# Two more tiles of x1 turned by VectorE in 32 by 32 blocks and by eight stores and two loads, instead of by TensorE

## The reference

```
x1  = layernorm(x  + causal_attention(x) @ Wo)              # 16 heads of 64, rotary positions
x2  = layernorm(x1 + softmax(x1 @ ctx^T) @ ctx)             # one head of 1024 features, per batch
out = layernorm(x2 + x2 @ W^T + bias + lora(x2))            # rank 16, an adapter chosen per batch
```

## Time and profile before

| | |
|---|---|
| median of 3 runs | 523.17 us (522.85 to 523.24) |
| profiled execution: its own time | 521.92 us |
| profiled execution: span, first to last instruction | 519.9 us |
| TensorE (PE) busy with matmuls | 511.7 us, 98% of the span |
| VectorE (DVE), ScalarE (ACT), GpSimd (POOL) busy | 324.4, 262.1 and 158.7 us |
| mean granted TensorE clock | 0.997 of full speed |
| packets of all transfers | 48358, of which 13224 under 512 bytes |

### The profile page before, as it was taken

One profiled execution on the slowest core, in us unless ns is written; L12 is line 12 of the kernel. 1 busy time (PEld: TensorE's weight loads), 2 busy tenths in 40 slices (PEclk: granted clock), 3 DMA queues, 4 the chain that ended last, 5 costly groups with the idle time before them and its releaser, 6 DMA issues.

```text
span 519.9 us, 7807 instructions
## 1 busy us (share of the span) xinstructions
PE 511.7 (98%) x2848; PEld 436.5 (84%) x2848; DVE 324.4 (62%) x695; ACT 262.1 (50%) x664; POOL 158.7 (31%) x142
## 2 busy tenths in 40 slices
PE   8999999999999999999999999999999999999995
PEld 5888888888989888888978888888787888888884
DVE  4742000177776868677774788778888786855432
ACT  5623210183846648384565356367767575535231
POOL 0003500536353554742005450115657010120010
PEclk9999999999999999999999999999999999999998
DMA  8907612431021111100097677579788685842011
GB/s 281 319 20 181 183 40 82 130 115 49 32 63 62 42 40 43 42 2 0 1 254 189 142 204 216 148 211 303 200 258 212 171 230 178 222 122 98 1 76 46
DMA packets 48358, 67.70 MB, mean 130 GB/s; under 512 B 13224, under 2 KB 31016, under 8 KB 48320
## 3 DMA queue, kind: packets, MB, share of 16 engines
q1 hardware_dynamic: 47648, 66.68, 44.9%
q10 hardware_dynamic: 672, 0.52, 0.3%
HBM read 55.13 MB, written 4.72 MB: 115 GB/s over the span
## 4 chain that ended last, share of the span: by engine, by line
PE 94%; DVE 2%; DMA 2%; ACT 1%; POOL 1%; issue 0%; SPq 0%; DVEq 0%; ACTq 0%
PE bank L576 30%; PE bank L693 28%; PE bank L587 15%; PE bank L783 6%; PE bank L603 3%; PE bank L618 3%; PE bank L814 2%; PE bank L816 2%; PE bank L819 2%; PE bank L755 1%; DMA cf_raw<-ctx_feat 1%; PE bank L767 1%; DMA x_raw<-x_feat 1%; PE bank L724 1%; PE bank L726 1%; PE bank L798 0%
## 5 line engine op out<-in xcount | busy, mean ns | idle before, releaser
L576 PE MATMUL bank<-x_hi,w_hi 128*128 128x512 f32 (+1 forms) x256 | 93.6, 365 | 0.0
L576 PE MATMUL bank<-x_hi,w_lo 128*128 128x512 f32 (+1 forms) x256 | 93.1, 364 | 0.0
L576 PE MATMUL bank<-x_lo,w_hi 128*128 128x512 f32 (+1 forms) x256 | 93.0, 363 | 0.0
L1435 DVE STREAM_TRANSPOSE prob_t<-prob 32x256 f32<-32x256 f32 x160 | 69.7, 436 | 12.1 <-ACT prob L989 9.4
L1819 POOL TENSOR_TENSOR w_lo<-w_mix,w_hi 128x1024 fp32r<-128x1024 f32 x16 | 38.3, 2395 | 104.5 <-ACT w_hi L961 104.5
L693 PE MATMUL bank<-wo,act_hi 128*128 128x512 f32 x224 | 70.2, 394 | 0.0
L693 PE MATMUL bank<-ffn,act_hi 128*128 128x512 f32 x224 | 69.7, 392 | 0.0
L979 ACT ACTIVATE prob<-prob,shift 112x112 f32<-112x112 f32 x128 | 47.8, 377 | 40.8 <-DVE shift L1418 40.8
L1832 POOL TENSOR_TENSOR norm<-norm,minus_half 128x1 f32<-128x1 f32 (+1 forms) x22 | 16.6, 754 | 135.5 <-DVE norm L1508 135.5
L576 PEld LDWEIGHTS bank<-x_hi,w_hi 128*128 128x128 f32 x256 | 48.1, 188 | 6.0
L576 PEld LDWEIGHTS bank<-x_lo,w_hi 128*128 128x128 f32 x256 | 48.1, 188 | 5.1
(11 more groups left out here) (123 smaller groups left out, 961.5 us busy)
## 6 DMA issues: line engine op xcount, KB each, us to landing
cf_raw<-ctx_feat SPq DMA_DIRECT2D x32, 376.0 KB, 4.7
ct_raw<-ctx_tok SPq DMA_DIRECT2D x24, 448.0 KB
w_raw<-qkv_w SPq DMA_DIRECT2D x16, 512.0 KB, 3.5
half_raw<-wo_w SPq DMA_DIRECT2D x16, 256.0 KB, 6.0
half_raw<-ffn_w SPq DMA_DIRECT2D x16, 256.0 KB, 6.6
wv_raw<-qkv_w SPq DMA_DIRECT2D x15, 256.0 KB, 7.4
x_raw<-x_feat SPq DMA_DIRECT2D x7, 448.0 KB, 8.2
out<-y_t SPq DMA_DIRECT2D x6, 512.0 KB, 4.4
```

The source lines that it names most:

```text
L576: last = pe.matmul(to[:, 0:cols.stop - cols.start], a[:, k, :], b[:, k, cols], start=(k == 0 and b is x_hi and a is w_hi[w]), stop=(k == K ...
L1435: return dve.transpose(quads(prob_t_wide[r], key, query), quads(prob_wide[r], query, key))
```

## The change

Tiles 5 and 6 of x1 take the way of the blocks too; batches 3 and 5 of x2 stay on it. `turn_tile(5)` and `turn_tile(6)` go from TensorE's list, and `round_turned` and `rest_turned` of a5 and a6 become `round_blocks` and `rest_blocks`.

- VectorE turns the blocks of tile 5, then later of tile 6, from `x_t[i % 4]` into `x_t[3]`, whose own tile has been used. It first waits that tile 3 has been read, and for tile 6 that the four stores of tile 5 have landed.
- Four stores of 128 KB per tile, each from 32 partitions and in runs of 32 elements (128 bytes), put the blocks in their turned places in DRAM, and one load of 512 KB in runs of 128 elements (512 bytes) brings the tile back into the bytes of `act_lo`, where ScalarE and VectorE make `act_hi` and `act_lo` of it.
- `keep_y(0, 0)` now also waits until tile 6's stores have landed.
- The lists of SyncE, ScalarE, VectorE and GpSimd are put in another order from about 340 us on. In SyncE's: the context rows of batch 2 ahead of the first `load_ff`, `load_cf(15)` and `load_cf(16)` ahead of `load_ff(6)` and `load_ff(7)`; `save_blocks("a5")` behind `load_cf(19)`, `load_blocks("a5")` ahead of `load_cf(22)`, `save_blocks("a6")` behind it and ahead of the context rows of batch 4; then `load_cf(23)`, `load_cf(24)`, the store of batch 3, and the load of tile 6.

```diff
-TURNS = ["a0", "a1", "a2", "b0", "a3", "b1", "a4", "b2", "a5", "a6", "b4", "b6", "b7"]
+TURNS = ["a0", "a1", "a2", "b0", "a3", "b1", "a4", "b2", "b4", "b6", "b7"]
-BLOCKS = [3, 5]
+BLOCKS = ["a5", "a6", "b3", "b5"]
...
+        act_raw = at("act_raw", [P, KT, B * S], A0 + 28672)
+        tile_blocks = x_t[3]
...
+            def save_blocks(name):
+                at_q, i = blocks_before(name), int(name[1:])
+                sp.wait_ge(swapped, at_q + 1)
+                if at_q:
+                    sp.wait_ge(saved, saved_after(BLOCKS[at_q - 1]))
+                if name[0] == "a":
+                    for q in range(QUADS):
+                        sp.dma_start(blocks_out[at_q][:, :, QUAD * q:QUAD * q + QUAD].rearrange(
+                                         "k (d r) t -> r (k d) t", d=QUADS),
+                                     tile_blocks[QUAD * q:QUAD * q + QUAD, :].rearrange(
+                                         "r (m t) -> r m t", t=QUAD)).then_inc(saved, 16)
...
+            def load_blocks(name):
+                at_q, i = blocks_before(name), int(name[1:])
+                sp.wait_ge(saved, saved_after(name))
+                if at_q:
+                    sp.wait_ge(moved, moved_after(BLOCKS[at_q - 1]))
+                if name[0] == "a":
+                    sp.dma_start(act_raw[:, :, tile_of(i)],
+                                 blocks_out[at_q].rearrange("k p t -> p k t")).then_inc(moved, 16)
...
             cross_mix(3)
-            turn_tile(5)
             ffn(1, 0, 4)
...
             cross_mix(4)
-            turn_tile(6)
             ffn(1, 1)
...
-                    act.wait_ge(turned, 2 * AT_TURN[f"a{i + 3}"] + 2)
+                    wait_tile_read(act, i + 3)
+                    if i == 0:
+                        act.wait_ge(saved, saved_after("a6"))
...
+            def swap_blocks(name):
+                i = int(name[1:])
+                if name[0] == "a":
+                    dve.wait_ge(x1_ready, i + 1)
+                    wait_tile_read(dve, 3)
+                    for b, which in copies_of(3):
+                        dve.wait_ge(row_in[which][b % ROWS], piece_in(b, which))
+                    if blocks_before(name):
+                        dve.wait_ge(saved, saved_after(BLOCKS[blocks_before(name) - 1]))
+                    dve.transpose(tile_blocks[:, :], x_t[i % 4][:, :]).then_inc(swapped, 1)
```

More of the change, by code:

```diff
@@ L316, in cf_before, with blocks_before, saved_after, moved_after @@
             return m - 3 if m < 7 else m - 2
-        def blocks_before(b):
-            return BLOCKS.index(b)
+        def blocks_before(name):
+            return BLOCKS.index(name)
+        def saved_after(name):
+            return sum(64 if n[0] == "a" else 16 for n in BLOCKS[:blocks_before(name) + 1])
+        def moved_after(name):
+            return sum(16 if n[0] == "a" else 64 for n in BLOCKS[:blocks_before(name) + 1])
+        def block_feat(name):
+            i = int(name[1:])
+            if name[0] == "a":
+                return act_raw[:, :, tile_of(i)], tile_of(i)
+            return x2_turned[i % ROWS][:, :, 0:S], tokens_of(i)
+        def wait_row_free(engine, b):
+            if f"b{b}" in BLOCKS:
+                engine.wait_ge(block_rest, 2 * blocks_before(f"b{b}") + 2)
+            else:
+                engine.wait_ge(turned, 2 * AT_TURN[f"b{b}"] + 2)
+        def wait_tile_read(engine, i):
+            if f"a{i}" in BLOCKS:
+                engine.wait_ge(swapped, blocks_before(f"a{i}") + 1)
+            else:
+                engine.wait_ge(turned, 2 * AT_TURN[f"a{i}"] + 2)
         def weight(of, n, k, part):
@@ L418, in copy_row @@
                              ).then_inc(row_in[which][b % ROWS], 16)
[L420 to L433, removed]
+            def save_blocks(name):
[9 more added lines that the diff above has]
+                                         "r (m t) -> r m t", t=QUAD)).then_inc(saved, 16)
+                else:
+                    sp.dma_start(blocks_out[at_q].rearrange("k p f -> p k f"),
+                                 x2_turned[i % ROWS]).then_inc(saved, 16)
@@ new lines, in load_blocks @@
+            def load_blocks(name):
[6 more added lines that the diff above has]
+                                 blocks_out[at_q].rearrange("k p t -> p k t")).then_inc(moved, 16)
+                else:
+                    for d in range(QUADS):
+                        sp.dma_start(x2_turned[i % ROWS][QUAD * d:QUAD * d + QUAD, :, :].rearrange(
+                                         "p k (q t) -> p (k q) t", q=QUADS),
+                                     blocks_out[at_q][:, :, QUAD * d:QUAD * d + QUAD].rearrange(
+                                         "k (q j) t -> j (k q) t", q=QUADS)).then_inc(moved, 16)
@@ L498, in _ @@
             load_ct(2, 2)
+            load_ff(0)
+            load_ff(1)
+            load_ff(2)
             load_ff(3)
@@ L544, in _ @@
             load_cf(29)
+            copy_row(6, 0)
+            copy_row(6, 1)
             copy_row(7, 0)
@@ L1241, in _ @@
             round_cf(19)
+            norm_x1(6)
             round_ff(11)
+            round_ct(23)
             round_cf(20)
@@ L1306, in _ @@
             round_ct(42)
+            norm_x2(6)
             round_ct(43)
-            norm_x2(6)
-            keep_y(3, 1)
             keep_cprob_t(7)
@@ L1313, in _ @@
             round_ct(46)
-            norm_y(3)
+            keep_y(3, 1)
             round_turned("b6")
             round_ct(47)
+            norm_y(3)
             keep_t_part(2)
@@ L1653, in _ @@
             add_wo(6)
+            rest_turned("a1")
             cross_top(0)
-            rest_turned("a1")
+            rest_ct(0)
             rest_cf(4)
-            rest_ct(0)
             rest_ct(1)
@@ L1701, in _ @@
             rest_cf(16)
+            cross_top(3)
+            add_wo(12)
+            rest_ct(17)
             rest_cf(17)
-            cross_top(3)
-            rest_ct(17)
-            add_wo(12)
             add_row(2)
```

181 lines of the change are left out of this document (91 added, 90 removed).

## The result

The changed kernel takes 525.18 us (median of 6 runs, 524.65 to 526.04); the kernel before, run beside it, takes 522.54 us. The ratio is 1.0054, with a 95% interval of 1.004 to 1.0067: slower by about 2.8 us. The forecast was 521.6 us, in a range that ended at 524.7. The profiled execution took 524.65 us, span 522.5 us at a mean granted clock of 0.995; that of before had a span of 519.9.

What follows compares the result with a forecast made beforehand. TensorE's list was taken as the bound (94% of the chain). -0.5 at `cross_score(5, last)`, -0.87 for tile 6 and -0.25 from 367 us gave -1.6 on the 523.17 median: 521.6 us, range 520.5 to 524.7.

Steps and rivals of the forecast that it cites:

- All hold: Other places fed by the queue, a5's tile, `keep_y(0, 0)`, batch 3's blocks: ready in time, each under a microsecond to spare.
- the rests change only their source, 0.65 us each as now: On VectorE: two more block turns of 1.24 us each, while the rests of a5 and a6 keep their 0.65 us.
- Nothing in the change leaves TensorE idle for long, so it costs nothing: TensorE's granted clock stays at 1.00, the 2.4 GHz level, with no cost.
- Two blocks, -1.74: Two eight-transpose blocks leave TensorE's list at 0.87 us each, the sure part of the gain.
- The queue: Transfers of 3.3 + 2.0 + 3.3 us delay `cf` part 23 to 411.5; `cross_score(5, last)` waits 0.8 us, starting at 413.3.
- The pause at `add_low`: At 401.81 us, TensorE's wait for VectorE's low-rank part shrinks from 0.72 to 0.3 us.
- The pause at 367 us: TensorE's wait for `cf` part 15, now rounded and loaded earlier: 0.25 of its 0.27 us gained.
- Rival 1: Transfers are hidden: stores overlap or cost 2.5 us, part 23 lands by 410.4; -2.4, 520.8 us, chance 0.15.
- rivals 3 and 4: Dearer transfers: each at its longest landing, 524.7 us, chance 0.11; short-run stores at double cost, 528.3 us, chance 0.07.
- Rival 2: Gain given back: part 23 lands at 412.6 or tile 6's stores delay `keep_y(0, 0)`; -0.5, 522.7 us, chance 0.27.
- rival 3: Three transfers each cost their longest landing, 11.7 us together; part 23 lands at 414.6; +1.5, 524.7 us, chance 0.11.
- the longest new pause stands elsewhere: Sign of being wrong: longest new pause at `cross_mix(3)` (VectorE), `ffn(0, 1)` (the bank) or `ffn(2, 0)` (batch 3's blocks).

Runs made afterwards that it cites:

- b3_first: Changed kernel with batch 3's four block loads ahead of two thirds of batch 5's context rows in SyncE's list: 523.97 us, ratio 1.0044.
- pool_in: Changed kernel with one added wait: VectorE lets GpSimd finish batch 4's scale and shift before the rest of tile 6: 521.88 us, ratio 0.9994.
- mended: Changed kernel with the edits of pool_in and b3_first, and the low-rank part kept and masked earlier: 523.02 us, ratio 1.0023, one 2919 us execution left out.
- same_again: The changed kernel word for word, measured once more: 524.28 us, ratio 1.0039 to the kernel before.
- long_runs: Changed kernel with stores of a5 and a6 in 512-byte runs, leaving out the moving of blocks within a tile: 522.95 us, ratio 1.0016.
- b3_last: Changed kernel with batch 3's four block loads behind the last third of batch 5's context rows: 525.53 us, ratio 1.0066.
- b3_ahead: b3_first with batch 3's blocks rounded and their rests taken ahead of batch 4's normalisation, GpSimd unprotected: 523.32 us, ratio 1.0018.
- pool_in_b3: Changed kernel with the edits of both pool_in and b3_first: 523.28 us, ratio 1.0015.

## Why the prediction was wrong

**The step that failed** is the sentence on batch 3's blocks: they "land near 426 and are ready near 428; `ffn(2, 0)` wants them at 429.86 - 0.5 - 0.87 = 428.5" and, of all of them, "All hold". I went from the landing straight to the rest and added 2 us, and left out what stands ahead of the rounding in ScalarE's list: `norm_x2(4)`, and with it GpSimd. The rest was done at 430.74 in place of 428, TensorE waited 2.11 us where I had none, and b3_first shows that a landing at 421.39 changes nothing in it. The landing was wrong too, 427.91 in place of 426. The held GpSimd operation hid that, but by itself it would have left about 1.1 us of the pause (see pool_in), so "All hold" would have failed without GpSimd as well.

Behind it is a smaller sentence: "the rests change only their source, 0.65 us each as now". Their own duration is as I had it (687 against 652 ns). But the source was what mattered, to a neighbour: from a bank to SBUF, and GpSimd's operation goes from 0.55 to 3.89 us. The trace of before had the sign: the same operation at line 1832 took 0.55 us as a rule and 1.84 us at 334.50. I priced the instruction and not what runs beside it.

**"Nothing in the change leaves TensorE idle for long, so it costs nothing"** fell with it: 1.59 us in the profiled execution. Over the executions: of twelve of b3_first five had a granted clock of 0.991 to 0.995 and spans of 522.9 to 525.3 us, seven had 0.996 to 0.999 and 520.9 to 522.0; of ten of pool_in, none was below 0.997. That the pause brings the fall is argued from this and from its place behind the pause in three profiles (the changed kernel, b3_first, mended); same_again, long_runs and b3_last have such a pause and no fall, and one of the twelve executions of b3_ahead, whose longest pause was 0.80 us, has a clock of 0.995. No run separates the two.

**The other terms.** Two blocks, -1.74: right, as the account shows. The queue: right. The share was 1.00 from 380 to 401 and 0.91 from 401 to 406 us, part 23 landed at 411.36 (predicted 411.5, of which the half microsecond to report stood on no row), and `cross_score(5, last)` started at 413.52 (413.3) after 0.79 us of pause (0.8). The stores cost what I had taken for them: in the trace 3.31 us of all 16 engines for a5's, 3.29 for the four loads that I took the price from. That the landing and the pause agree to 0.15 us is partly luck, since the other executions without an edit ahead of it (see the table) have 411.5 to 413.0 and 0.65 to 1.74 us. Windows after:

```profile
380.00:401.00 21.00, 20.72 (x109) 17.51 (x107) 15.53 (x31) 13.24 (x23) 14.43 (x14) 1.00 1.00 256
401.00:406.00 5.00, 4.53 (x24) 4.09 (x25) 4.90 (x12) 4.01 (x7) 1.88 (x3) 1.00 0.91 202
```

The pause at `add_low` was to shrink from 0.72 to 0.3 us and grew to 0.83. VectorE took the kept part at 399.75, as foreseen (399.5) and 1.37 us earlier than before, but TensorE came at 400.56, not at 401.2: I had taken off the block and left out the 0.27 and 0.17 us of pauses that went as well. As foreseen, part 23 hid it. a5's rest came 0.31 us late. The pause at 367 us went, as predicted, in this profile, but 0.17 to 0.66 us of it stand in nine of the eleven other profiles with the change (0.24 in same_again), so that this gain came in full was luck.

**The rivals.** Rival 1, hidden transfers, and rivals 3 and 4, dearer ones, did not come: the stores cost what loads in the same runs do. Rival 2's later landing, 412.6, came about in some executions, but the loss stood at another place. The time came out near rival 3's 524.7, but not by its mechanism. Of the three places that I named for "the longest new pause stands elsewhere", it is the third, `ffn(2, 0)`, but the cause that I wrote beside it, batch 3's blocks, is not what ended the pause, as b3_first shows.

In sum: forecast -1.6 us, measured +2.6 between the two profiles, so 4.2 us to explain. Of these 0.5 stand ahead of `cross_score(5, last)`, which moved by -0.26 us where the sum has -0.5 - 0.25: 0.22 of the difference is the later start (413.52, not 413.3), and the 0.25 us from 367 us should not have been counted, since part 23 sets the time there, the reason for which I let the 0.3 us of `add_low` drop out. The new pause at `ffn(2, 0)` is 2.11, and the clock behind it 1.59.

## What to carry to other kernels

When an edit changes where an operand lies, look not only at that instruction's duration but at what another engine runs beside it: a tiny GpSimd operation on a path to TensorE should not meet a run of VectorE instructions with both operands in SBUF, and one wait that keeps them apart can pay. The sign is in a trace of the kernel before: the same small operation with durations far apart. The held time is listed as busy, not as idle. When asking whether data are ready in time, walk the consumer's in-order list back from the instruction that needs them, not forward from the landing: what stands ahead of it there may be the late one. Where two things are late, the later hides the other, which comes to light only when the first is mended. And moving a load forward moves lateness to what it passed, as pool_in_b3 shows.

## What the runs showed of the hardware that I had not expected

- A GpSimd TENSOR_TENSOR of 112 numbers: 0.55 us beside a VectorE instruction that reads a bank; 1.84 us beside two with both operands in SBUF (1.53 us of work), 3.89 beside five (3.6 us), 4.96 beside seven (4.7 us). It ends 0.4 us behind the run in all three. But it is not always held through a whole run: at 371.33 us of the changed kernel it ended, at 372.33, 0.4 us behind the first of two and beside the second. What decides that, these traces don't show. GpSimd's and VectorE's timelines after:

```profile
371.33 1.00 POOL L1901 TENSOR_TENSOR norm<-norm,minus_half 128x1 f32<-128x1 f32 x1 [0.38 <-DVE norm L1564]
```

```profile
371.23 0.68 DVE L1655 TENSOR_TENSOR ct_lo<-ct_raw,ct_hi 125x512 fp32r<-125x512 f32 x1
371.83 0.94 DVE L1662 TENSOR_TENSOR cf_lo<-cf_raw,cf_hi 128x752 fp32r<-128x752 f32 x1
```

- Stores of 128-byte runs are priced like loads of them: for 512 KB 3.31 us of all 16 engines against 3.29 for loads, and 1.74 for stores in 512-byte runs. They also hold SyncE: the four of a5 take 5.4 us to issue, one of them 3.76 us.
- After a pause of 2.1 to 2.3 us the granted clock fell to its 1.2 GHz level for some 3.5 us in three profiled executions and not in three others, one of them of the same kernel.
